# Seven block products in place of eight for the last half of a shared expert, with weight sums on GpSimd

## Chip, cores and metric

The kernel runs on one core of one Trainium2 chip. The metric is the device time of one execution in microseconds; lower is better. All values are fp32; products run as fp32r with each operand split into a high and a low part.

## What is computed

An attention-like recurrence with layer norm, then a mixture of experts with a shared expert, then a layer norm again. The change lies in the shared expert's first matrix product, `x @ w_sh_gate_up`. There are 2048 tokens of 512 numbers and 8 experts, 2 of them for each token; the shared expert goes from 512 to 2 x 1024 (gate and up) and back to 512; `_silu_and_mul` is silu of the first half times the second.

```python
x = _layernorm(x + _L0_attn_ref(x, ...), axis=-1)
x = _layernorm(x + _L0_ffn_ref(x, ...), axis=-1)
...
gu = jnp.einsum('th,ehf->etf', x, w_gate_up)
act = _silu_and_mul(gu)
eo = jnp.einsum('eti,eih->eth', act, w_down)
routed = jnp.einsum('te,eth->th', combine, eo)
shared = _silu_and_mul(x @ w_sh_gate_up) @ w_sh_down
return (routed + shared).reshape(orig_shape)
```

## The kernel before

`stages()` writes out one plan, a list of steps; the five functions `sync`, `tensor`, `vector`, `scalar` and `gpsimd` each run through it and issue their own part of each step, so that every engine's queue has the plan's order. Semaphore waits by name (`on`) tie the engines together.

The tokens are 16 tiles of 128, in four groups q of 512. A unit w holds weights for 256 inner columns: gate columns and up columns of w_gate_up, 128 at a time (fc 0 and 1), and the matching rows of w_down. Units 0 to 3 are the shared expert for groups 0 and 1, then come 15 routed jobs (w = 4 to 18; eight of them full ones of 512 rows, seven strips that are run only if used), and units BASE to BASE+3 (w = 19 to 22) are the shared expert again, for groups 2 and 3.

A weight or activation x is split as high = fp32r(x) on ACT and low = x - high on DVE (gate weights, tokens, activations) or POOL (down weights); a product is three products, high*high, high*low, low*high (`TERMS`). For one unit and group, `gate` gives for each fc a gate half and an up half, each 4 contraction chunks x 3 terms = 12 products of 128x128 by 128x512 (L1181); `act` is silu on ACT (L1671), the multiply on DVE (L1454), the high part on ACT (L1673) and the low part on DVE (L1456). `down` is four tiles of 6 products (L1194), each added to the token tile in x1 by DVE (L1464). PSUM banks 0 to 3 take gate halves, 4 to 7 the down tiles.

The experts' results lie in DRAM (yd), stored by SP after a copy on ACT (L1724). For each token tile POOL fetches two rows per token by indirect DMA (`fetch`, L1828; two buffers, so fetch i+2 waits for join i), and DVE multiplies and adds them (`join`, two operations, L1512). `finish` takes the mean and variance (L1522, L1524 and three small POOL operations), `scale` applies them on ACT (L1729; the last tile on DVE, L1529), and SP stores the tile.

The end of the routed jobs: `rows_gate(14)` (w = 18, 48 products, L1268), in it the split of unit 19's gate weights (`split_gate`, L1652, L1444) after fc 0; one strip of `rows_down(13)`; twelve products of `gate(BASE, 2)`; `rows_down(14)` (24 products, L1305); then the eight unit and group pairs of `seq`, with joins and finishes from `jobs` between the gate's steps:

```python
    first = gate(BASE, 2)
    next(first)
    next(first)
    rows_down(JOBS - 1, iter(()))
...
            if step % 2 == 0:
                scale()
                if n in jobs:
                    (join if jobs[n][0] == "join" else finish)(jobs[n][1] + step // 2)
```

## Time and profile before

| | us |
|---|---|
| median of 3 runs (lowest, highest) | 688.53 (687.93, 689.41) |
| the profiled execution | 688.28 |
| its span, first to last instruction | 686.5 |

| engine | busy us | share | instructions |
|---|---|---|---|
| PE | 666.1 | 97% | 6828 |
| DVE | 425.4 | 62% | 745 |
| ACT | 294.3 | 43% | 510 |
| POOL | 294.3 | 43% | 308 |

PE is TensorE, DVE VectorE, ACT ScalarE, POOL GpSimd, SP the engine that issues most DMAs. A group of instructions is told by its source line, as L1194. A product's recorded duration (0.39 us for 512 columns) is longer than the distance between starts, since products overlap; what a product costs is read from the distance. The granted clock of TensorE is 1.00 where it runs at 2.4 GHz.

### The profile page before, as it was taken

To read this page: it belongs to the slowest core of one execution; us is meant where nothing else is said; L and a number is where in the kernel's file an instruction comes from. 1 tells how busy PE (TensorE), PEld (TensorE's weight loads), DVE (VectorE), ACT (ScalarE), POOL (GpSimd) and SP (SyncE) were. 2 spreads that over 40 slices of the span, in tenths; PEclk is the share of its full clock that TensorE was granted. 3 is DMA by queue.
4 is the path that set the end of the run, shared out by engine and by line. 5 is a ranking of instruction groups with operands and counts; after the bars stand their busy time and mean duration, and the time that the engine had idled before them with its cause. 6 is when DMAs were issued, how large, how long until landed. Compare 5 with 4: busy or idle time off the path is not lost.

```text
span 686.5 us, 16409 instructions
## 1 busy us (share of the span) xinstructions
PE 666.1 (97%) x6828; PEld 531.9 (77%) x6828; DVE 425.4 (62%) x745; ACT 294.3 (43%) x510; POOL 294.3 (43%) x308
## 2 busy tenths in 40 slices
PE   9999999999999999999999999999999999999994
PEld 7767777677777777787887888888887888888883
DVE  5875865876844464488946544554456267676655
ACT  5343444455454432531023656655667442142232
POOL 0747567667645431011015335533552244726232
PEclk9999999999999999999999999999999999999998
DMA  8213234232642441100064478676748765414222
GB/s 286 83 35 86 76 98 106 88 112 57 175 138 75 129 141 33 46 0 1 21 231 157 140 292 295 214 220 255 216 153 271 229 218 159 123 66 131 65 78 92
DMA packets 65998, 92.47 MB, mean 135 GB/s; under 512 B 16960, under 2 KB 32064, under 8 KB 65920
## 3 DMA queue, kind: packets, MB, share of 16 engines
q1 hardware_dynamic: 60240, 72.76, 32.2%
q0 software_dynamic: 5680, 18.62, 9.4%
q8 instruction: 56, 0.92, 0.6%
q14 instruction: 22, 0.18, 0.1%
HBM read 67.56 MB, written 23.79 MB: 133 GB/s over the span
## 4 chain that ended last, share of the span: by engine, by line
PE 67%; DVE 14%; POOL 8%; issue 6%; ACT 4%; DMA 1%; POOLq 0%; DVEq 0%; ACTq 0%
PE zbank L1181 8%; PE wbank L1181 7%; PE bank L1305 7%; PE bank L1194 7%; PE bank L1073 7%; PE zbank L1268 6%; PE wbank L1268 6%; PE bank L1128 4%; DVE x L1464 3%; PE zbank L1281 2%; PE bank L1181 2%; PE wbank L1107 2%; PE zbank L1091 2%; POOL za L1758 2%; DVE sg L1454 1%
## 5 line engine op out<-in xcount | busy, mean ns | idle before, releaser
L1790 POOL TENSOR_TENSOR xl<-RAW,xh 128x1024 fp32r<-128x1024 f32 x23 | 55.4, 2407 | 121.1 <-ACT xh L1657 120.9
L1673 ACT ACTIVATE ah<-sg 128x512 fp32r<-128x512 f32 x48 | 30.3, 632 | 157.4 <-DVE sg L1454 157.4
L1803 POOL DMA_INDIRECT xg<-x1d,idxu x39 | 42.1, 1079 | 71.2 <-DVE idxu L889 41.3
L1444 DVE TENSOR_TENSOR GL<-RAW,GH 128x1024 fp32r<-128x1024 f32 x42 | 50.3, 1223 | 11.2 <-ACT GH L1652 9.8
L1456 DVE TENSOR_TENSOR al<-sg,ah 128x512 fp32r<-128x512 f32 x48 | 34.2, 712 | 33.5 <-ACT ah L1673 33.5
L1194 PE MATMUL bank<-xh,ah 128*128 128x512 f32 x128 | 51.3, 401 | 2.3 <-DVE x L1464 1.9
L1828 POOL DMA_INDIRECT xg<-yd,SI x32 | 35.8, 1120 | 40.0 <-DVE x L1512 23.6
L1194 PE MATMUL bank<-xh,al 128*128 128x512 f32 x128 | 50.0, 390 | 0.0
L1194 PE MATMUL bank<-xl,ah 128*128 128x512 f32 x128 | 49.9, 390 | 0.0
L1073 PE MATMUL bank<-xh,GH 128*128 128x512 f32 x112 | 47.9, 427 | 0.8 <-DVE kS L1346 0.8
L1454 DVE TENSOR_TENSOR sg<-sg,zbank 128x512 f32<-128x512 f32 x22 | 15.1, 685 | 53.4 <-PE zbank L1268 36.4
L1652 ACT ACTIVATE GH<-RAW 128x1024 fp32r<-128x1024 f32 x44 | 45.2, 1056 | 0.0
L1464 DVE TENSOR_TENSOR x<-bank,x 128x512 f32<-128x512 f32 x64 | 40.9, 681 | 5.5 <-PE bank L1194 5.3
L1073 PE MATMUL bank<-xl,GH 128*128 128x512 f32 x112 | 44.1, 394 | 0.2
L1181 PE MATMUL zbank<-XH,GH 128*128 128x512 f32 x112 | 44.1, 394 | 0.2 <-DVE XL L1449 0.2
L1181 PE MATMUL wbank<-XH,GH 128*128 128x512 f32 x112 | 43.8, 391 | 0.0
L1073 PE MATMUL bank<-xh,GL 128*128 128x512 f32 x112 | 43.7, 390 | 0.0
L1181 PE MATMUL zbank<-XH,GL 128*128 128x512 f32 x112 | 43.6, 389 | 0.0
L1181 PE MATMUL wbank<-XH,GL 128*128 128x512 f32 x112 | 43.6, 389 | 0.0
L1181 PE MATMUL wbank<-XL,GH 128*128 128x512 f32 x112 | 43.6, 389 | 0.0
L1181 PE MATMUL zbank<-XL,GH 128*128 128x512 f32 x112 | 43.6, 389 | 0.0
L1512 DVE SCALAR_TENSOR_TENSOR x<-xg,WW,x 128x512 f32<-128x512 f32 x32 | 26.6, 841 | 14.3 <-DMA xg<-yd,SI 12.6
(301 smaller groups left out, 1753.6 us busy)
## 6 DMA issues: line engine op xcount, KB each, us to landing
RAW<-in_wgu SPq DMA_DIRECT2D x13, 1024.0 KB, 5.8
yd<-RAW SPq DMA_DIRECT2D x39, 256.0 KB, 5.2
RAW<-in_wsgu SPq DMA_DIRECT2D x14, 512.0 KB, 4.8
RAW<-in_wd SPq DMA_DIRECT2D x13, 512.0 KB, 5.8
xr<-in_xT SPq DMA_DIRECT2D x16, 256.0 KB, 4.7
x<-in_xtok SPq DMA_DIRECT2D x16, 256.0 KB, 4.2
x1d<-x SPq DMA_DIRECT2D x16, 256.0 KB, 2.5
RAW<-in_wsd SPq DMA_DIRECT2D x8, 512.0 KB, 4.5
```

The source lines that it names most:

```text
L1073: t = e.matmul(bank[b][:], (WL if wl else WH)[:, j, k, hg * 128:hg * 128 + 128], (xl if xlo else xh)[:, k, :], start=(k == 0 and not wl an ...
L1181: t = e.matmul(bank[b][:], (GL if wl else GH)[:, w % 2, k, c:c + 128], (XL if xlo else XH)[q % 2][:, k, :], start=(k == 0 and not wl and n ...
L1194: t = e.matmul(bank[b][:], (al if al_ else ah)[:, ap, k, j * 128:j * 128 + 128], (DL if wl else DH)[:, w % 2, k, :], start=(k == 0 and not ...
L1268: t = e.matmul(bank[b][:], (GL if wl else GH)[:, w % 2, k, c:c + 128], (rowl if xlo else rowh)[p][:, k, :], start=(k == 0 and not wl and n ...
L1305: t = e.matmul(bank[b][:], (al if al_ else ah)[:, p, k, h * 128:h * 128 + 128], (DL if wl else DH)[:, w % 2, k, :], start=(k == 0 and not ...
L1444: e.tensor_tensor(GL[:, w % 2, k:k + 2, :], gate_raw(w, k), GH[:, w % 2, k:k + 2, :].bitcast(F32), ALU.subtract).then_inc(*mark("low", "g" ...
L1456: e.tensor_tensor(al[:, ap, fc, :], sg[:, g, :], ah[:, ap, fc, :].bitcast(F32), ALU.subtract).then_inc(*mark("low", "a", w, q, fc))
L1464: e.tensor_tensor(x1[:, i, :], bank[b][:], x1[:, i, :], ALU.add).then_inc(*mark("acc", w, q, j))
L1652: e.activation(GH[:, w % 2, k:k + 2, :], gate_raw(w, k), ACT.Copy).then_inc(*mark("high", "g", w, k))
L1790: e.tensor_tensor(DL[:, w % 2, :, :], draw[:, raw_of(w), :, :], DH[:, w % 2, :, :].bitcast(F32), ALU.subtract).then_inc(*mark("low p", "d" ...
L1803: e.indirect_dma_start(place(s), None, x1d, bass.IndirectOffsetOnAxis(ap=idxu[:, LINES[s]:LINES[s] + 1], axis=0)).then_inc(*mark(f"dma xg{ ...
L1828: e.indirect_dma_start(xg[:, p, j, :], None, yd, bass.IndirectOffsetOnAxis(ap=SI[:, j, i:i + 1], axis=0)).then_inc(*mark(f"dma ya{p}", i, j))
```

## The change

Tokens of group 2 and 3, two halves of the contraction (chunks 0 and 1, 2 and 3), and gate and up columns form a 2 x 2 by 2 x 2 block product. It is computed by Strassen's scheme in Winograd's form, one block for each unit and fc (b = 0 to 7), with seven products of 2 chunks x 3 terms = 6 matmuls each (`SEVEN`: weight slot, token operand, bank, and whether it opens the bank) for what were eight.

- Token sums (T1 to T4, once): four differences and one sum of 1024 elements a partition on DVE (`pair sums`), high parts on ACT, low parts on DVE (`pair sums`, `pair splits`). Group 2's tokens are loaded again (`fetch pair`); group 3's are loaded one job earlier.
- Weight sums (four of 256 elements, for each block): on POOL (`mix sums`), high parts on ACT (`mix high`, `mix high sums`), low parts of plain weights on DVE and of sums on POOL (`mix low`). They take the place of `split_gate`.
- Result sums: the products accumulate in banks 0 to 3. Where a partial result is needed in two banks it is copied on ACT (`copy 1`, `copy 2`, `copy 5`), and DVE adds (`add 5`, `add 7`). `pair act` is `act` for both groups.
- `down` tiles go one by one between the products of a block (order 1, 5, 6, 2, 7, 3, 4; a tile after 5, 2, 3 and 4), a unit later; block 0 has the order 1, 2, 5, 6, 7, 3, 4 and lies among `rows_down(13)` and `rows_down(14)`, block 1 has no tiles among it. Joins and finishes are placed by `side`. Tiles 12 to 15 are finished before 8 to 11, and tile 11 is the last.
- Buffers are laid over others that are free by then; some activations of group 3 go to the y buffers (`y_done`).

```diff
+SEVEN = {1: (0, "B11", 0, True), 2: (1, "B21", 0, False), 3: (6, "B22", 1, False), 4: (2, "T4", 2, False),
+         5: (3, "T1", 3, True), 6: (4, "T2", 1, False), 7: (5, "T3", 2, False)}
...
                 if j + 1 < JOBS:
                     for _ in turn_rows(j + 1):
                         pass
-                split_gate(j + 5)
+                    split_gate(j + 5)
+                else:
+                    mix(0, gate_end[w - 1])
+                    do("pair sums")
+    mul_end, act_end = {}, {}
+    def mix(b, after):
+        do("mix sums", b, after)
+        do("mix high", b, after)
+        do("mix high sums", b)
+        do("mix low", b)
+    def block(b, order):
+        w, fc = BASE + b // 2, b % 2
+        for p in order:
+            do("mul", b, p, left[SEVEN[p][2]] if SEVEN[p][3] else None)
+            mul_end[b] = ("mul", b, p)
+            if p == 1:
+                do("copy 1", b, left[1])
+            elif p == 5:
+                do("copy 5", b)
+            elif p == 6:
+                do("copy 2", b, left[2])
+                do("add 5", b)
+            elif p == 2:
+                do("silu 2", b)
+                left[0] = ("silu", w, 2, fc)
+            elif p == 7:
+                do("add 7", b)
+            elif p == 3:
+                do("pair act", b, 3, ("down", w - 2, 3, 3) if b > 3 else None)
+                left[1], left[3] = ("silu", w, 3, fc), ("low", "a", w, 3, fc)
+            elif p == 4:
+                do("pair act", b, 2, ("down", w - 1, 2, 3) if b > 1 else None)
+                left[2] = ("low", "a", w, 2, fc)
+            yield p
+    def pair_down(u, q):
+        w = BASE + u
+        for j in range(4):
+            b, i = 4 + j, 4 * q + j
+            do("down", w, q, j, b, (2 if u % 2 else 1) if q == 3 else 0, left[b], acc.get(i))
+            acc[i] = left[b] = ("acc", w, q, j)
+            down_end[w] = ("down", w, q, j)
+            yield i
 
...
+        if j == JOBS - 3:
+            do("fetch pair")
         do("load down", j + 6)
         between = iter(())
         if ORDER[j] < FULL:
             rows_gate(j)
-            do("load gate", j + 7)
+            if j < JOBS - 1:
+                do("load gate", j + 7)
         else:
             between = rows_and_weights(j)
             next(between)
             strip_gate(j)
+            if j == JOBS - 2:
+                do("fetch tokens", 3, row_left[1], range(4))
             for _ in range(3):
                 next(between)
         if j == JOBS - 1:
-            do("fetch tokens", 3, row_left[1], range(4))
+            do("pair splits", gate_end[4 + j])
+            first = block(0, (1, 2, 5, 6, 7, 3, 4))
+            next(first)
         if j:
             rows_down(j - 1, between)
         if ORDER[j] >= FULL:
         split_down(j + 5)
 
 
-    first = gate(BASE, 2)
-    next(first)
-    next(first)
-    rows_down(JOBS - 1, iter(()))
-    seq = [(BASE + n, q) for n, q in ((0, 2), (0, 3), (1, 2), (1, 3), (2, 2), (3, 2), (2, 3), (3, 3))]
-    jobs = {1: ("join", 0), 2: ("join", 4), 3: ("finish", 0), 4: ("join", 8), 5: ("join", 12), 6: ("finish", 4), 7: ("finish", 8)}
...
+    def among():
+        yield
+        next(first)
+        yield
+        next(first)
+        yield
+    next(first)
+    rows_down(JOBS - 1, among())
+    mix(1, gate_end[4 + JOBS - 1])
+    split_down(BASE + 1)
+    do("load gate", BASE + 2)
+    do("load down", BASE + 2)
     do("fetch", 0)
     do("fetch", 1)
...
+    for _ in first:
+        pass
+    side = {1: (("join", 0), ("join", 1), ("join", 2)), 2: (("join", 3), ("join", 4), ("join", 5)),
+            3: (("join", 6), ("join", 7), ("finish", 0), ("finish", 1)), 4: (("join", 8), ("join", 9), ("finish", 2), ("finish", 3)),
+            5: (("join", 10), ("join", 11), ("join", 12)), 6: (("join", 13), ("join", 14), ("join", 15)),
+            7: (("finish", 4), ("finish", 5), ("finish", 6), ("finish", 7))}
+    for b in range(1, 8):
+        u = b // 2
+        downs = pair_down(u - 1, 2 + b % 2) if u else iter(())
+        jobs = iter(side[b])
+        for p in block(b, (1, 5, 6, 2, 7, 3, 4)):
+            if p == 1 and b < 7:
+                do("mix sums", b + 1, mul_end[b - 1])
+                do("mix high", b + 1, mul_end[b - 1])
+            if p == 1 and b in (4, 6):
+                split_down(BASE + u)
+            if p == 2 and b < 7:
+                do("mix high sums", b + 1)
+                do("mix low", b + 1)
+            if p in (1, 6, 2, 3):
                 scale()
...
+                kind, i = next(jobs, (None, 0))
+                if kind:
+                    (join if kind == "join" else finish)(i)
+            if p in (5, 2) or p in (3, 4) and b < 7:
+                next(downs, None)
+        if b == 2:
             do("load gate", BASE + 3)
             do("load down", BASE + 3)
...
+    scale()
+    for _ in downs:
+        pass
+    for i in pair_down(3, 3):
+        finish(i)
+        scale(keep=1)
+    for i in pair_down(3, 2):
         finish(i)
         scale(keep=1)
...
+                elif step == "mul":
+                    b, p, free = a
+                    s, name, to, opens = SEVEN[p]
+                    if free:
+                        e.wait_ge(*on(*free))
+                    if p in (1, 2):
+                        e.wait_ge(*on("low", "m", b, 0))
+                    elif p == 4:
+                        e.wait_ge(*on("low", "m", b, 2))
+                    else:
+                        e.wait_ge(*on("low p", "m", b))
+                    if b == 0:
+                        e.wait_ge(*(on("low", "f", 2, 3) if name in ("B11", "B21") else on("low", "pair", name)))
+                    if p == 6:
+                        e.wait_ge(*on("copied", b, 1))
+                    elif p == 2:
+                        e.wait_ge(*on("copied", b, 1))
+                    elif p == 7:
+                        e.wait_ge(*on("copied", b, 2))
+                    elif p == 3:
+                        e.wait_ge(*on("added", b, 5))
+                    elif p == 4:
+                        e.wait_ge(*on("added", b, 7))
+                    for k in range(2):
+                        for wl, xlo in TERMS:
+                            t = e.matmul(bank[to][:], mixed(GL if wl else GH, b, s)[:, k, :], tokens_of(name, xlo)[:, k, :],
+                                         start=(opens and k == 0 and not wl and not xlo), stop=True, skip_group_check=True)
+                    t.then_inc(*mark("mul", b, p))
...
+                elif step == "pair sums":
+                    q1, q2 = pairs_[:, 0, :, :], pairs_[:, 1, :, :]
+                    r1, r2, t2 = XL1_[:, 0:2, :], XL1_[:, 2:4, :], xg_[:, 1, :, :]
+                    e.wait_ge(*on("dma pair", 3))
+                    e.wait_ge(*on("dma xr1", 3, 3))
+                    e.tensor_tensor(q1, r1, q1, ALU.subtract).then_inc(*mark("pair sum", 1))
+                    e.tensor_tensor(q2, q2, r2, ALU.subtract).then_inc(*mark("pair sum", 0))
+                    e.wait_ge(*on("pair sum", 1))
+                    e.tensor_tensor(r1, r2, r1, ALU.subtract).then_inc(*mark("pair sum", 3))
+                    e.wait_ge(*on("turned", "r", len(LINES) - 1))
+                    e.tensor_tensor(t2, r2, q1, ALU.subtract).then_inc(*mark("pair sum", 2))
+                    e.wait_ge(*on("pair sum", 0))
+                    e.tensor_tensor(q2, q2, q1, ALU.add).then_inc(*mark("pair sum", 4))
+                    e.wait_ge(*on("high", "pair", "T3"))
+                    for name in ("B22", "T3"):
+                        e.tensor_tensor(tokens_of(name, True), r1 if name == "T3" else r2, tokens_of(name, False).bitcast(F32), ALU.subtract).then_inc(*mark("low", "pair", name))
+                elif step == "pair splits":
+                    for name, raw in (("T1", pairs_[:, 0, :, :]), ("T2", xg_[:, 1, :, :]), ("T4", pairs_[:, 1, :, :])):
+                        e.wait_ge(*on("high", "pair", name))
+                        e.tensor_tensor(tokens_of(name, True), raw, tokens_of(name, False).bitcast(F32), ALU.subtract).then_inc(*mark("low", "pair", name))
+                elif step == "add 5":
+                    b, = a
+                    e.wait_ge(*on("mul", b, 6))
+                    e.wait_ge(*on("copied", b, 2))
+                    e.tensor_tensor(bank[1][:], bank[1][:], turned[:], ALU.add).then_inc(*mark("added", b, 5))
+                elif step == "add 7":
+                    b, = a
+                    e.wait_ge(*on("mul", b, 7))
+                    e.wait_ge(*on("added", b, 5))
+                    e.tensor_tensor(bank[3][:], bank[2][:], turned[:], ALU.add).then_inc(*mark("added", b, 7))
...
+                elif step == "mix high":
+                    b, after = a
+                    e.wait_ge(*on(*gate_in(BASE + b // 2)))
+                    e.wait_ge(*on(*after))
+                    e.activation(mixed(GH, b, 0, 2), graw[:, raw_of(BASE + b // 2), :, 128 * (b % 2):128 * (b % 2) + 128], ACT.Copy).then_inc(*mark("high", "m", b, 0))
+                    e.activation(mixed(GH, b, 2), quarter(3, b), ACT.Copy).then_inc(*mark("high", "m", b, 2))
+                elif step == "mix high sums":
+                    b, = a
+                    e.wait_ge(*on("mixed", b, 4))
+                    e.activation(mixed(GH, b, 3, 4), mixed(GL_, b, 3, 4), ACT.Copy).then_inc(*mark("high", "m", b, 3))
+                elif step == "pair sums":
+                    e.wait_ge(*on("pair sum", 3))
+                    e.wait_ge(*on("gate", 4 + JOBS - 2, "r", 0, 1))
+                    for name in ("B22", "T3"):
+                        e.activation(tokens_of(name, False), XL1_[:, 0:2, :] if name == "T3" else XL1_[:, 2:4, :], ACT.Copy).then_inc(*mark("high", "pair", name))
+                elif step == "pair splits":
+                    gone, = a
+                    e.wait_ge(*on(*gone))
+                    e.wait_ge(*on("pair sum", 4))
+                    e.activation(tokens_of("T1", False), pairs_[:, 0, :, :], ACT.Copy).then_inc(*mark("high", "pair", "T1"))
+                    e.activation(tokens_of("T2", False), xg_[:, 1, :, :], ACT.Copy).then_inc(*mark("high", "pair", "T2"))
+                    e.wait_ge(*on("low", "pair", "T1"))
+                    e.activation(tokens_of("T4", False), pairs_[:, 1, :, :], ACT.Copy).then_inc(*mark("high", "pair", "T4"))
+                elif step == "copy 1":
+                    b, free = a
+                    e.wait_ge(*on("mul", b, 1))
+                    e.wait_ge(*on(*free))
+                    e.activation(bank[1][:], bank[0][:], ACT.Copy).then_inc(*mark("copied", b, 1))
+                elif step == "copy 5":
+                    b, = a
+                    e.wait_ge(*on("mul", b, 5))
+                    if b:
+                        e.wait_ge(*on("added", b - 1, 7))
+                    e.activation(turned[:], bank[3][:], ACT.Copy).then_inc(*mark("copied", b, 5))
...
+                elif step == "mix sums":
+                    b, after = a
+                    e.wait_ge(*on(*gate_in(BASE + b // 2)))
+                    e.wait_ge(*on(*after))
+                    s1, s2, s3, s4 = (mixed(GL_, b, 3 + n) for n in range(4))
+                    e.tensor_tensor(s1, quarter(2, b), quarter(3, b), ALU.add).then_inc(*mark("mixed", b, 1))
+                    e.tensor_tensor(s3, quarter(0, b), quarter(2, b), ALU.subtract).then_inc(*mark("mixed", b, 3))
+                    e.wait_ge(*on("mixed", b, 1))
+                    e.tensor_tensor(s2, s1, quarter(0, b), ALU.subtract).then_inc(*mark("mixed", b, 2))
+                    e.wait_ge(*on("mixed", b, 2))
+                    e.tensor_tensor(s4, quarter(1, b), s2, ALU.subtract).then_inc(*mark("mixed", b, 4))
+                elif step == "mix low":
+                    b, = a
+                    e.wait_ge(*on("high", "m", b, 3))
+                    e.tensor_tensor(mixed(GL, b, 3, 4), mixed(GL_, b, 3, 4), mixed(GH, b, 3, 4).bitcast(F32), ALU.subtract).then_inc(*mark("low p", "m", b))
```

## Rows read from the trace of the kernel before

**Rows 1.** Page, busy us (share of the span) and instructions of each engine.

```profile
PE 666.1 (97%) x6828; PEld 531.9 (77%) x6828; DVE 425.4 (62%) x745; ACT 294.3 (43%) x510; POOL 294.3 (43%) x308
```

**Rows 2.** Chain that ended last, in time: start us, us, what; around the hand-over.

```profile
535.11 5.45 PE wbank L1268 x24
540.70 2.81 PE zbank L1181 x12
543.51 5.44 PE bank L1305 x24
```

**Rows 3.** Timeline of DVE at the hand-over: start us, us, engine, line, operation, tiles.

```profile
535.22 0.69 DVE L1454 TENSOR_TENSOR sg<-sg,zbank 128x512 f32<-128x512 f32 x1 [4.46 <-PE zbank L1268]
536.60 0.69 DVE L1456 TENSOR_TENSOR al<-sg,ah 128x512 fp32r<-128x512 f32 x1 [0.70 <-ACT ah L1673]
...
540.66 0.69 DVE L1454 TENSOR_TENSOR sg<-sg,wbank 128x512 f32<-128x512 f32 x1 [0.75 <-PE wbank L1268]
```

**Rows 4.** Timeline of ACT at the hand-over.

```profile
536.48 1.99 ACT L1652 ACTIVATE GH<-RAW 128x1024 fp32r<-128x1024 f32 x2
...
551.18 0.60 ACT L1724 ACTIVATE RAW<-bank 128x512 f32<-128x512 f32 x1 [2.96 <-DMA yd<-RAW]
```

**Rows 5.** Groups by shape on DVE, 500 to 687 us: busy, mean ns, idle before.

```profile
L1444 DVE TENSOR_TENSOR GL<-RAW,GH 128x1024 fp32r<-128x1024 f32 x14 | 16.7, 1221 | 1.8 <-ACT GH L1652 1.6
...
L1504 DVE TENSOR_TENSOR al<-wbank,ah 128x256 fp32r<-128x256 f32 x2 | 0.9, 426 | 0.9 <-ACT ah L1718 0.9
```

**Rows 6.** Groups by shape on ACT, 500 to 687 us.

```profile
L1673 ACT ACTIVATE ah<-sg 128x512 fp32r<-128x512 f32 x21 | 13.3, 632 | 73.7 <-DVE sg L1454 73.7
...
L1724 ACT ACTIVATE RAW<-bank 128x512 f32<-128x512 f32 x15 | 9.2, 616 | 6.6 <-PE bank L1305 3.6 <-DMA yd<-RAW 3.0
```

**Rows 7.** Groups by shape on POOL, whole span.

```profile
L1790 POOL TENSOR_TENSOR xl<-RAW,xh 128x1024 fp32r<-128x1024 f32 x23 | 55.4, 2407 | 121.1 <-ACT xh L1657 120.9
...
L1752 POOL TENSOR_TENSOR xl<-xr,xh 128x512 fp32r<-128x512 f32 x2 | 2.5, 1276 | 1.2 <-ACT xh L1595 1.2
```

**Rows 8.** One line's instructions, L1512: duration ns min/median/max, first and last start.

```profile
L1512 DVE SCALAR_TENSOR_TENSOR x<-xg,WW,x x32: 743/752/2887, 561.8 to 641.0; 128x512 f32<-128x512 f32 x32
```

**Rows 9.** Timeline of POOL, 555 to 572 us.

```profile
555.92 1.13 POOL L1828 DMA_INDIRECT xg<-yd,SI  x1 [10.00 <-DMA yd<-RAW]
...
561.62 2.54 POOL L1790 TENSOR_TENSOR xl<-RAW,xh 128x1024 fp32r<-128x1024 f32 x1
565.85 1.23 POOL L1828 DMA_INDIRECT xg<-yd,SI  x1 [1.68 <-DVE x L1512]
567.38 0.94 POOL L1828 DMA_INDIRECT xg<-yd,SI  x1 [0.30 <-issue]
...
570.21 0.95 POOL L1828 DMA_INDIRECT xg<-yd,SI  x1 [0.30 <-issue]
```

**Rows 10.** Timeline of DVE, 561 to 573 us.

```profile
561.83 2.89 DVE L1512 SCALAR_TENSOR_TENSOR x<-xg,WW,x 128x512 f32<-128x512 f32 x1
...
571.08 1.61 DVE L1512 SCALAR_TENSOR_TENSOR x<-xg,WW,x 128x512 f32<-128x512 f32 x2 [2.00 <-DMA xg<-yd,SI]
```

**Rows 11.** Windows: stretch, us, busy (x) PE, PEld, DVE, ACT, POOL, clock, DMA, GB/s.

```profile
677.50:680.00 2.50, 0.00 (x0) 0.00 (x0) 1.82 (x5) 1.55 (x2) 1.66 (x6) 1.00 0.52 201
681.00:684.00 3.00, 0.00 (x0) 0.00 (x0) 0.00 (x0) 0.00 (x0) 0.00 (x0) 0.50 0.44 169
```

**Rows 12.** Timeline of PE at the kernel's start.

```profile
1.46 4.05 PE L1058 MATMUL bank<-colsum 128*128 128x128 f32 x20 [1.46 <-DVE colsum L1320]
...
5.96 0.49 PE L1073 MATMUL zbank<-xh,GL 128*128 128x512 f32 x1
6.29 0.40 PE L1073 MATMUL zbank<-xh,GH 128*128 128x512 f32 x1
```

**Rows 13.** Timeline of DVE at the end.

```profile
676.30 0.66 DVE L1464 TENSOR_TENSOR x<-bank,x 128x512 f32<-128x512 f32 x1
...
677.82 0.66 DVE L1464 TENSOR_TENSOR x<-bank,x 128x512 f32<-128x512 f32 x1
```

More of the change, by code:

```diff
@@ L540, in sb, with under @@
             return stack.enter_context(nc.sbuf_tensor(name, [128] + shape, dt))
+        def under(name, shape, dt=F32):
+            with ExitStack() as brief:
+                return sb(brief, name, shape, dt)
         pair = [ctx.enter_context(nc.psum_tensor(n, [128, 2, 512], F32)) for n in ("zbank", "wbank")]
@@ L1460, in vector @@
                     e.wait_ge(*on("down", w, q, j))
+                    if before and w > BASE:
+                        e.wait_ge(*on(*before))
                     if not before and j == 0:
```

128 lines of the change are left out of this document (91 added, 37 removed).

## The prediction

> **What bounds the kernel now.** I read the page's busy shares first, then the chain that ended last in order of time, then the timelines of DVE, ACT and POOL around the place where the experts end and the shared expert's last half begins, then the groups by shape for durations.
>
> TensorE is busy 97% of the span with 6828 products [rows 1]. In the last 137 us the chain runs almost wholly over PE: 24 products in 5.44 us, product after product [rows 2]. That is 0.2267 us each, so six products, one "block product" of the new scheme or one `down` tile, take 1.36 us; I call that T. The gates of the last expert (w = 18) end at 540.56, twelve gate products of unit BASE fill the time until the expert's `act` is ready, and `rows down` follows with no hole [rows 2]. DVE starts 0.11 us after the last product of a half [rows 2, 3]; an engine released by ACT or DVE starts within 0.05 us. So each product taken from PE is worth its 0.2267 us as long as no other engine's queue makes PE wait. The question is what the queues of ACT, DVE and POOL, which run strictly in the plan's order, do with the added work.
>
> **Part 1, the products.** Before, units BASE to BASE+3 take 48 gate products for each of two token groups: 8 x 48 = 384. After: 8 blocks x 7 x 6 = 336. `down` is the same (192), so 48 products go: 48 x 0.2267 = **-10.9 us**, all of it on PE's path. This is the whole gain.
>
> **Part 2, the hand-over from the last expert.** Inside `rows_gate(14)`, between `act` of fc 0 and `act` of fc 1, the split of BASE's gate weights is replaced by `mix(0)` and `pair sums`; then `pair splits` comes before `copy 1` of block 0. Product 2 of block 0 waits for `copy 1`. PE has only product 1 and one `rows down` strip before it. So PE waits for all that stands ahead of `copy 1` on ACT, and that waits for DVE in its turn. Step by step, each duration from its row:
> - DVE ends fc 0's `low` at 537.3 [rows 3]. ACT begins `mix high` at 536.5, where the weight split stood [rows 4]: 0.6, 0.4, and 1.05 for the sums (two of 1024 take 1.99 [rows 4]), to 538.4. DVE's own `mix low`: 0.7 and 0.4 [rows 3, 5], to 538.3.
> - DVE, `pair sums`: five subtractions or additions of 1024 elements, 1.22 each alone [rows 5], 1.14 when they overlap (my estimate from that row less the 0.09 by which DVE operations overlap): the third ends at 541.7, the fifth at 544.0. ACT copies B22 and T3 behind the third: to 543.7. DVE takes their low parts, 2.3: to 546.2.
> - Only now does DVE reach fc 1's multiply, which before it did at 540.7: 0.69 [rows 3], to 546.9. ACT's high part 0.63 [rows 6]: 547.5. `pair splits`: T1 high 1.05, 548.5; T1 low on DVE 1.23, 549.8; T4 high, which waits for it, 1.05, 550.8; `copy 1` 0.6 [rows 6], 551.4.
> - PE is through product 1 and the strip at about 542.1. It waits 9.3 us.
>
> In the same stretch POOL runs `mix low(0)`, a subtraction of 1024 elements, 2.4 us [rows 7], against DVE's `pair sums`. The trace has such a meeting: POOL's subtraction from 561.62 to 564.16, and a DVE operation with both inputs in SBUF that started at 561.83 and took 2.89 us where the median is 0.75; it ended 0.6 after POOL [rows 8 to 10]. So I add 2.4 us: **+11.7 us**, and PE goes on at R = 553.8. (Bounds 9.3 and 12.5, the latter if `mix sums(0)` too falls on DVE.) The Trainium skill, SBUF — State Buffer, section Who interferes with whom, states that a DVE instruction with two SBUF inputs contends with a GpSimd instruction that reads SBUF, the loser blocking wholly; by that rule, and the trace agrees (2.89 us against 0.75), moving the weight sums to GpSimd doesn't make them free for DVE. Without it this term would be 9.3.
>
> **Part 3, the first joins.** `side` puts join 0, 1, 2 into block 1, which has no `down` tiles: 7T = 9.5 us. On DVE, `add 5` of block 1 is queued behind join 0 and `add 7` behind join 2; product 3 waits for the first, product 4 for the second. Fetch 2 on POOL needs join 0, and POOL has `mix sums(2)` ahead of it. From R:
> - PE needs 7 products or tiles to end `rows down(14)`: R + 9.5. ACT's `mix high(1)`, after one of the y copies (0.6, [rows 6]), ends by R + 12.0; POOL `mix low(1)` 2.4 and `split down` 2.4: R + 16.8. The last y store lands sooner: before, its copy ran at 551.18 and the fetch began at 555.92 [rows 4, 9], here R + 14.4.
> - Four fetch issues take 5.3 us (565.85 to 571.16, [rows 9]), and a tile is usable 3.7 us after its second issue starts (567.38 to 571.08, [rows 9, 10]): join 0 can start at R + 21.7, POOL has issued fetch 1 at R + 22.1.
> - `mix sums(2)`: four operations of 256 elements. POOL takes 1.28 for 512 and 2.41 for 1024 [rows 7], hence about 0.71 for 256: 2.9 us; with join 0's two operations of 0.75 on the other side of the lock, R + 26.5. Fetch 2's second issue starts at R + 27.8, lands R + 31.4, join 2 to R + 33.0, `add 7` to R + 33.7.
> - Product 4 of block 1 is the 17th piece after R: 16T = 21.8. PE waits 33.7 - 21.8 = **+11.9 us**. Check on the trace: from the first fetch to join 2 my steps need 14.6 us, and before it was 555.92 to 571.08 = 15.2 [rows 9, 10], where other gate products covered it. Bounds: 9 (no lock, split and sums partly overlapped) and 14.
>
> **Part 4, the blocks with `down` tiles.** 11T = 15.0 us each. Most waits fit: a copy costs 0.11 + 0.6 + 0.05, under T, and DVE's `add` 0.11 + 0.69 + 0.05. What does not is again `add 7` behind the third join (blocks 2, 5, 6). From the block's start: `mix sums` and the join under the lock 4.5, second issue 1.3, landing 3.7, join 1.6, one `acc` 0.7, `add 7` 0.7 = 12.5 against 9T = 12.2 for product 4; in block 6 `split down` (2.4) stands ahead of the fetch as well. Block 2 starts with POOL in arrears. I take 1.5 + 0.3 + 2.7 = **+4.5 us** (0 to 9).
>
> **Part 5, TensorE's clock.** PE is done by 677.5; the granted clock is 1.00 until 680 and 0.50 (1.2 GHz) from 681 to 684 [rows 11]. Both long holes are longer than the time between. At the kernel's start PE is busy from 1.46, and the 512-column products of 5.96 and 6.29 still start 0.33 apart in place of 0.227 [rows 12]. Half speed over such a stretch costs at most 2.4 us. I take 2.0 for the first hole; the second return partly lies under block 2's join chain, 1.0: **+3.0 us** (0 to 4.8).
>
> **Part 6, the end.** Eight tiles are finished one by one in place of four. DVE needs 1.52 us a tile (676.30 to 677.82, [rows 13]), PE 1.36: 4 x 0.16 = **+0.6 us**. The last tile has the same steps behind it. SP's token fetch goes one job earlier, ahead of four y stores, by 1.9 us of issue; the next copies that need their slots are over 10 us later: nothing. The pair loads go when SP is idle between weight loads: nothing. The added sums need no PE.
>
> **Sum.** The profiled execution took 688.28 (span 686.5 and 1.8 around it), 0.25 under the median of 688.53, so I use 688.3: 688.3 - 10.9 + 11.7 + 11.9 + 4.5 + 3.0 + 0.6 = 709.1. I forecast **709.0 us**. All low bounds: 688.3 - 10.9 + 9.3 + 9 = 695.7; all high: 688.3 - 10.9 + 12.5 + 14 + 9 + 4.8 + 0.6 = 718.3.
>
> **The rivals.**
> - Only the hand-over stalls; joins and fetches keep ahead of PE, as they do now. For it: in the trace PE never waits for a join. Against: there the accumulations do not stand behind joins on DVE. Time: 688.3 - 10.9 + 11.7 + 2.0 + 0.6 = 691.7. Chance 0.08.
> - Faster. The mechanism: ACT and DVE do the token sums while PE is still in `rows_gate(14)`, so that `copy 1` follows product 1 at once and the join chain starts with the present lead. It decides at a total stall of 10.9 us: below that the change gains. The price left is about 3 us of short waits: 688.3 - 10.9 + 3 = 680.4. Against: those sums begin only after 538 and hold some 13 us of dependent work. Chance 0.07.
> - GpSimd as the bound. In a block with three joins POOL has 2.9 + 2.4 of arithmetic and 3 x 2.65 of fetches, 13.3 of 15.0 us, and DVE some 12 us; if their lock serializes most of it, each of three such blocks loses 4 us more: 721. Chance 0.05.
> - No lock between DVE and POOL: 709.1 - 2.4 - 1.5 - 1.0 = 704.2, inside my case (0.15 of its 0.80).
>
> **How the numbers follow.** The forecast case holds 0.80, from 695.7 to 718.3. The range reaches to the first rival, since the two large terms could each be one I mis-ordered: 691 to 719, leaving out the faster case and the GpSimd case, and the ends. A measurement of this kernel tells about 0.2% (1.4 us) from no change. Faster 0.07, same 0.02, slower 0.91.
>
> **What would show it.** After: 6780 products on PE. In the chain, a hole before block 0's product 2 of about 11 us that ends with ACT's `copy 1` (its releaser), DVE in `pair sums` until about 548, and fc 1's multiply some 8 us later than 540.7. A hole of about 12 us in block 1 before product 4, released by DVE's `add 7`, with join 2 just ahead of it and, before that, the fetch's landing. Granted clock 0.5 behind both. DVE operations with two SBUF inputs far over their medians where POOL computes. The prediction is wrong if PE goes on within 3 us of 542, or if joins stand idle-free ahead of the additions.

## The result, and the profile after the change

The kernel after takes **718.75 us** (median of 4 runs, 718.25 to 719.6) against 688.23 (687.93 to 689.41) before: a ratio of 1.044 [1.042, 1.046]. The change costs 30.5 us, where its 48 products fewer are worth 10.9. The forecast was 709.0, in a range from 691 to 719; the sign and the two main places were right. The size fell at the range's end, 0.4 us above the sum of all high bounds (718.3).

The page of after (engine, busy us, share, instructions; then the slices), against [rows 1]:

```profile
PE 663.9 (93%) x6780; PEld 528.3 (74%) x6780; DVE 453.7 (63%) x775; ACT 318.2 (44%) x551; POOL 336.5 (47%) x348
...
PE   9999999999999999999999999999993939997893
...
PEclk9999999999999999999999999999997888999997
```

PE has its 6780 products, and two slices at 3 tenths. The waits of PE (who waited for what: us in all, times, longest) hold them; before, no gate product of the last 140 us was on that list:

```profile
PE wbank L1333 <- DVE wbank L1645: 16.1, 4, 9.1
PE zbank L1333 <- ACT zbank L1896: 11.7, 2, 11.5
PE zbank L1333 <- DVE zbank L1640: 3.2, 1, 3.2
```

L1333 is the product, L1896 `copy 1`, L1640 `add 5`, L1645 `add 7`. The timeline of PE at the holes (start, us, line, what ended the idle time; a hole is counted from 0.2267 us after the start of the last product before it, so it is a little longer than its bracket, since a matmul's shown end reaches beyond that). The first hole is put at 11.4 us throughout, with its two 32-column matmuls counted as long as full ones, though they take some 0.15 together:

```profile
541.34 0.40 PE L1333 MATMUL zbank<-XH,GL 128*128 128x512 f32 x1
541.58 0.30 PE L1465 MATMUL bank<-ident 128*128 128x32 f32 x2
553.39 0.77 PE L1333 MATMUL zbank<-XH,GH 128*128 128x512 f32 x1 [11.51 <-ACT zbank L1896]
553.95 0.63 PE L1333 MATMUL zbank<-XL,GH 128*128 128x512 f32 x1
554.38 0.63 PE L1333 MATMUL zbank<-XH,GL 128*128 128x512 f32 x1
...
581.19 0.47 PE L1333 MATMUL zbank<-XH,GH 128*128 128x512 f32 x1 [3.19 <-DVE zbank L1640]
...
591.95 1.19 PE L1333 MATMUL wbank<-pairs,GH 128*128 128x512 f32 x2 [9.14 <-DVE wbank L1645]
...
657.91 0.59 PE L1333 MATMUL wbank<-pairs,GH 128*128 128x512 f32 x1 [4.61 <-DVE wbank L1645]
...
676.90 0.47 PE L1333 MATMUL wbank<-pairs,GH 128*128 128x512 f32 x1 [2.14 <-DVE wbank L1645]
```

**The hand-over** (first hole, 11.4 us). DVE there, in the order of the plan:

```profile
537.97 1.22 DVE L1621 TENSOR_TENSOR pairs_<-XL_,pairs_ 128x1024 f32<-128x1024 f32 x1
539.11 3.42 DVE L1622 TENSOR_TENSOR pairs_<-pairs_,XL_ 128x1024 f32<-128x1024 f32 x1
...
545.85 2.35 DVE L1631 TENSOR_TENSOR XL<-XL_,XH 128x1024 fp32r<-128x1024 f32 x2
548.12 0.68 DVE L1605 TENSOR_TENSOR sg<-sg,wbank 128x512 f32<-128x512 f32 x1
```

The pair sums run from 538 to 548.1, and only then comes fc 1's multiply, 7.5 us after its time in [rows 3]. The second sum took 3.42 us in place of 1.22: POOL's subtraction lay beside it, itself 3.19 in place of the 2.41 of [rows 7]. On ACT, behind fc 1's high part, T1's, T2's and T4's high parts follow, T4's after T1's low part, and `copy 1` starts at 552.66:

```profile
538.25 3.19 POOL L2067 TENSOR_TENSOR GL<-GL_,GH 128x1024 fp32r<-128x1024 f32 x1 [1.80 <-ACT GH L1878]
...
551.70 1.06 ACT L1891 ACTIVATE pairs<-pairs_ 128x1024 fp32r<-128x1024 f32 x1 [0.34 <-DVE RL L1635]
552.66 0.58 ACT L1896 ACTIVATE zbank<-zbank 128x512 f32<-128x512 f32 x1
```

**Block 1** (3.3 and 9.3 us). DVE goes join 0, `add 5`, join 1, then sits 3.85 us until fetch 2 has landed, joins, and adds:

```profile
578.12 2.31 DVE L1715 SCALAR_TENSOR_TENSOR x<-xg,WW,x 128x512 f32<-128x512 f32 x2 [4.39 <-DMA xg<-yd,SI]
580.36 0.69 DVE L1640 TENSOR_TENSOR zbank<-zbank,turned 128x512 f32<-128x512 f32 x1
...
587.62 3.58 DVE L1715 SCALAR_TENSOR_TENSOR x<-xg,WW,x 128x512 f32<-128x512 f32 x2 [3.85 <-DMA xg<-yd,SI]
591.11 0.69 DVE L1645 TENSOR_TENSOR wbank<-wbank,turned 128x512 f32<-128x512 f32 x1
```

POOL issued that fetch (second issue at 583.97) behind four weight sums, which took 4.3 us beside the joins; alone they were put at 2.9. Join 2 itself took 3.58 us in place of 1.60, with POOL's `mix low(2)` beside it from 587.43 to 589.78:

```profile
577.95 0.73 POOL L2058 TENSOR_TENSOR GL_<-RAW 128x256 f32<-128x256 f32 x1
...
581.09 1.20 POOL L2063 TENSOR_TENSOR GL_<-RAW,GL_ 128x256 f32<-128x256 f32 x1
...
583.97 0.95 POOL L2107 DMA_INDIRECT xg<-yd,SI  x1 [0.30 <-issue]
```

**Where the 30.3 us of span went** (716.8 less 686.5): hand-over 11.4; block 1 12.6; blocks 5 and 6 4.8 and 2.3; products slower than 0.2267 apart, and holes up to 0.5 us, 8.3 in all; the end 1.8 (from the last product to the last `scale` 5.28 us, 3.49 before); less 10.9. That adds to 30.3. The windows (stretch, us, busy and count of PE, PEld, DVE, ACT, POOL, granted clock, DMA share, GB/s) show the clock behind the holes, where before has 1.00 in both stretches:

```profile
553.40:562.00 8.60, 8.60 (x26) 6.87 (x27) 0.61 (x1) 3.28 (x6) 5.16 (x5) 0.67 0.18 68
592.00:600.00 8.00, 8.00 (x26) 6.41 (x27) 4.48 (x7) 3.18 (x6) 5.47 (x7) 0.71 0.25 68
```

### The profile page after: what moved, and what is told of

Same layout as the page of the kernel before. It is cut to its first block, busy times and chain, and to the rows that moved or that the text cites. A ratio compares the mean times of both kernels' runs of the same rounds, so it can differ in the third digit from the quotient of the medians.

```text
span 716.8 us, 16598 instructions
## 1 busy us (share of the span) xinstructions
PE 663.9 (93%) x6780; PEld 528.3 (74%) x6780; DVE 453.7 (63%) x775; ACT 318.2 (44%) x551; POOL 336.5 (47%) x348
## 4 chain that ended last, share of the span: by engine, by line
PE 64%; DVE 15%; POOL 8%; issue 7%; ACT 4%; DMA 1%; DVEq 0%; POOLq 0%; ACTq 0%
PE bank L1456 7%; PE bank L1345 7%; PE bank L1196 6%; PE zbank L1419 6%; PE wbank L1419 5%; PE zbank L1333 4%; PE bank L1251 4%; PE wbank L1333 4%; PE zbank L1304 3%; PE wbank L1304 3%; PE zbank L1432 2%; PE wbank L1230 2%; PE bank L1304 2%; PE zbank L1214 2%; POOL za L2020 1%
## 5 line engine op out<-in xcount | busy, mean ns | idle before, releaser
L1935 ACT ACTIVATE ah<-sg 128x512 fp32r<-128x512 f32 x32 | 20.2, 632 | 97.1 <-DVE sg L1605 97.1
L1595 DVE TENSOR_TENSOR GL<-RAW,GH 128x1024 fp32r<-128x1024 f32 x34 | 40.9, 1224 | 10.7 <-ACT GH L1855 9.3
L1345 PE MATMUL bank<-xh,ah 128*128 128x512 f32 x112 | 45.0, 402 | 2.0 <-DVE x L1667 1.8
L2107 POOL DMA_INDIRECT xg<-yd,SI x32 | 32.1, 1003 | 16.8 <-DVE x L1715 9.8
L1715 DVE SCALAR_TENSOR_TENSOR x<-xg,WW,x 128x512 f32<-128x512 f32 x32 | 31.7, 991 | 12.3 <-DMA xg<-yd,SI 10.6
L1607 DVE TENSOR_TENSOR al<-sg,ah 128x512 fp32r<-128x512 f32 x32 | 24.2, 756 | 22.3 <-ACT ah L1935 22.3
L1855 ACT ACTIVATE GH<-RAW 128x1024 fp32r<-128x1024 f32 x36 | 37.2, 1059 | 0.0
L1792 ACT ACTIVATE W<-wbank 128x512 f32<-128x512 f32 x31 | 18.5, 597 | 37.8 <-PE wbank L1230 37.8
L1538 DVE TENSOR_TENSOR r<-zbank,mask 128x256 f32<-128x256 f32 x31 | 13.0, 419 | 33.9 <-PE zbank L1214 33.6
L1333 PE MATMUL zbank<-XH,GH 128*128 128x512 f32 x48 | 19.9, 414 | 14.7 <-ACT zbank L1896 11.5
L2020 POOL TENSOR_TENSOR za<-r 128x512 f32<-128x512 f32 x16 | 24.4, 1523 | 18.3 <-ACT r L1785 16.5
L1230 PEld LDWEIGHTS wbank<-r,RAW 32*32 32x32 f32 x2048 | 22.3, 103 | 12.7 <-issue 11.3
```

What stands on the lines that cost most here:

```text
L1230: t = e.matmul(bank[2 + h][g:g + 32, pp * 64:pp * 64 + 64], KK[o:o + 32, par, 1, c:c + 32], r[o:o + 32, n // 2 % 2, n % 2, 256 * h + pp * ...
L1333: t = e.matmul(bank[to][:], mixed(GL if wl else GH, b, s)[:, k, :], tokens_of(name, xlo)[:, k, :], start=(opens and k == 0 and not wl and ...
L1345: t = e.matmul(bank[b][:], act_of(al if al_ else ah, ap, k)[:, j * 128:j * 128 + 128], (DL if wl else DH)[:, w % 2, k, :], start=(k == 0 a ...
L1595: e.tensor_tensor(GL[:, w % 2, k:k + 2, :], gate_raw(w, k), GH[:, w % 2, k:k + 2, :].bitcast(F32), ALU.subtract).then_inc(*mark("low", "g" ...
L1855: e.activation(GH[:, w % 2, k:k + 2, :], gate_raw(w, k), ACT.Copy).then_inc(*mark("high", "g", w, k))
```

## Experiments

Times are compared with the kernel before on the same chip (688.1 to 689.3), so 1 us between runs of different chips is not read.

**e1_fill**: what the clock costs. PE is kept busy with products into a bank that nobody reads.

```
+ for _ in range({(0, 2): 48, (1, 4): 38}.get((b, p), 0)):
+     e.matmul(bank[4][:], mixed(GH, b, 0)[:, 0, :], ..., start=True, stop=True)
  if free:
      e.wait_ge(*on(*free))
```

> The changed kernel, with 48 extra products on TensorE (into a bank that nobody reads) ahead of block 0's product 2 and 38 ahead of block 1's product 4, where PE stands idle for 11.4 and 9.3 us. Nothing else moves. Theory (the slow products behind the two holes, 0.43 us apart, are the lower granted clock): they start 0.227 apart again, 2.9 us are won behind the first hole and 2.3 behind the second: 713.5 us, granted clock 1.00 in both places. Rival (the slow products come from their operands or from the queues): the spacing stays at 0.43 and the time at 718.7.

Measured 715.51, ratio 1.038 [1.034, 1.042]. The product after the filled hole is at normal pace at once:

```profile
554.12 0.47 PE L1335 MATMUL zbank<-XH,GH 128*128 128x512 f32 x1 [0.55 <-ACT zbank L1898]
554.43 0.40 PE L1335 MATMUL zbank<-XL,GH 128*128 128x512 f32 x1
554.66 0.40 PE L1335 MATMUL zbank<-XH,GL 128*128 128x512 f32 x1
```

The same work between the first hole and the second takes 21.5 us in place of 24.2, and between block 1's long hole and block 5's 58.7 in place of 61.0: the clock took **2.7 and 2.3 us**. The unfilled holes keep their size (3.4, 4.8, 2.3). The profiled run as a whole is only 2.0 us shorter than after's. It reached the hand-over 0.7 later; the second filling outlasted `add 7` (done at 589.96, product 4 at 590.79) by 0.7; and behind block 6's hole of 2.3 us the products ran 0.43 apart from 674.5 to 677.5 (granted clock 0.66 from 675.6 to 679.0), which costs 1.4 us and is not there in after, behind the same hole. So a lower clock can follow short holes too, and filling two holes does not take its whole price away.

**e2_zero**: what POOL's subtraction does to DVE. The low part of the weight sums is set to zero, so it is left out of the output; POOL still writes it, but reads nothing.

```
- e.tensor_tensor(mixed(GL, b, 3, 4), mixed(GL_, b, 3, 4), mixed(GH, b, 3, 4).bitcast(F32), ALU.subtract)
+ e.memset(mixed(GL, b, 3, 4).bitcast(F32), 0.0)
```

> The changed kernel, with POOL's subtraction for the low part of the weight sums replaced by a fill with zeros of the same 1024 elements, which reads no SBUF (the low part of the weight sums is left out of the computation). Theory (POOL reading SBUF locks DVE operations with two SBUF inputs): the second operation of pair sums falls from 3.42 to 1.22 us, the first hole from 11.4 to about 9.2, the two long joins of 2.9 in blocks 1 and 5 to 0.75: about 712 us. Rival (POOL's low part costs DVE nothing, only the queue order counts): 3.42 stays or the time stays at 718. Rival (writing alone takes the port too): the same as now.

Measured 707.01, ratio 1.026 [1.020, 1.032]: 12 us less than after, five more than expected.

```profile
538.57 0.96 POOL L2067 MEMSET GL<- 128x1024 f32 x1 [1.75 <-ACT GH L1878]
...
539.45 1.22 DVE L1622 TENSOR_TENSOR pairs_<-pairs_,XL_ 128x1024 f32<-128x1024 f32 x1
```

The same DVE operation takes 1.22 us beside a POOL instruction that only writes. The hand-over's hole is 9.2 (9.3 was forecast without the lock), block 1's are 2.0 and 7.3, block 5's 0.8 in place of 4.8. So the lock's price is 2.2 us in the hand-over, as the prediction had it, but some 7 in the blocks, where it had 1.5 and 1.0 (the terms of its rival without a lock). The memset is shorter too (0.96 for 2.4 us of POOL), so the blocks' share is not all lock, and no run parts the two. The two runs lie 3.4 us apart (705.32 and 708.70). The Trainium skill, SBUF — State Buffer, section Who interferes with whom, has the conflict in the port pair that VectorE and GpSimd share; the runs agree, 1.22 beside a GpSimd operation that reads nothing and 3.42 beside one that reads two inputs.

**e3_joins**: joins moved. Block 1 has none ahead of its additions; in blocks 2 to 6 the one behind product 1 still stands ahead of `add 5` on DVE, which product 3 waits for, so the expectation's "none ... within the block" holds for `add 7` alone.

```
- side = {1: (("join", 0), ("join", 1), ("join", 2)), 2: ...
+ side = {1: {4: ("join", 0)}, 7: {...}}
+ for b in range(2, 7):
+     side[b] = {1: ("join", 3 * b - 5), 7: ("join", 3 * b - 4), 4: ("join", 3 * b - 3)}
```

> The changed kernel, only the joins placed otherwise: none before block 1's last product, then in each block one after product 1, one behind add 7, one behind the last act, so that none stands on DVE ahead of an addition that a product waits for within the block. Theory (the holes of blocks 1, 5 and 6, 19.7 us, and the clock they cost, 4.3, come from additions queued behind joins that wait for a fetch): about 695 us, the first hole unchanged at 11.4. Rival (the fetches themselves are the bound, 16 joins need their time wherever they stand): over 708 us, with holes in front of the last tiles.

Measured 711.46, ratio 1.032 [1.029, 1.035]. A miss by 16 us (695 expected); the time lies in the rival's range (over 708), though not with holes ahead of the last tiles alone. Block 1's two holes of 12.6 us went, for one of 2.8 at the head of block 2, but seven of 0.7 to 2.3 us stand in blocks 4 to 7, 9.4 in all, where after has 7.1 in two. One cause that the prediction had not named, here for the hole at the head of block 2: ACT's `mix high sums` waits for POOL's weight sums, which stand behind fetch issues, and token group 3's `silu` in `pair act` is queued behind it, with DVE's multiply behind that. (ACT waits there in six blocks, 19.5 us in all.) Timelines of POOL, ACT and DVE:

```profile
575.93 1.07 POOL L2107 DMA_INDIRECT xg<-yd,SI  x1 [0.30 <-issue]
577.02 0.75 POOL L2058 TENSOR_TENSOR GL_<-RAW 128x256 f32<-128x256 f32 x1
...
580.01 1.06 ACT L1878 ACTIVATE GH<-GL_ 128x1024 fp32r<-128x1024 f32 x1 [3.81 <-POOL GL_ L2063]
580.97 0.58 ACT L1921 ACTIVATE sg<-zbank 128x512 f32<-128x512 f32 x1
...
581.58 0.70 DVE L1651 TENSOR_TENSOR wbank<-sg,wbank 128x512 f32<-128x512 f32 x1 [3.92 <-ACT sg L1921]
```

**e4_hand**: the hand-over re-placed. The pair sums are cut into single steps (`s` a sum, `h` a high part, `l` a low part), placed behind `act` of fc 1 and between the `rows down` strips.

```
- mix(0, gate_end[w - 1]); do("pair sums")
+ mix(0, gate_end[w - 1])
...
+ pair("s1", "hT1", "s2")
  rows_down(JOBS - 1, among())    # among: hT2 lT1 lT2 s3 | hT3 s0 lT3 | s4 hB22 ...
```

> The changed kernel, only the hand-over placed otherwise: copy 1 directly behind block 0's product 1, the token sums and their splits cut into single steps and put behind the last expert's act, between its down tiles, and block 0's products 5 and 6 after the third of them; the down split of unit 19 after block 0. Theory (queue order makes the first hole of 11.4 us and costs 2.9 of clock): the hole falls under 2 us in sum, block 1's holes stay at 12 to 13: 704 us. Rival (DVE and ACT have too much work in the hand-over whatever the order): over 4 us of holes remain between 542 and 558: 709 or more.

Measured 714.37, ratio 1.037 [1.034, 1.040]: 10 us over the expectation. The hole of 11.4 became 6.5 in seven pieces, but block 1's grew to 5.5 and 8.3:

```profile
563.59 4.69 POOL L2065 TENSOR_TENSOR xl<-RAW,xh 128x1024 fp32r<-128x1024 f32 x2 [5.11 <-ACT xh L1876]
568.42 0.96 POOL L2120 DMA_INDIRECT xg<-yd,SI  x1
```

PE reaches block 1's first hole 7.0 us sooner than in after (570.7 against 577.6), but the first fetch, with two `down` splits ahead of it, only 4.8 (568.42 against 573.22), and PE leaves block 1's long hole 4.8 us sooner too (587.16 against 591.95). The rest of what the hand-over gives is waited for in block 1.

**e5_dve**: weight sums and low parts on DVE, so that POOL has only fetches and `down` splits. The plan's order is unchanged; the two branches move, word for word, from POOL's loop to DVE's.

```
- POOL: "mix sums" (4 x 256 elements), "mix low" (1024)
+ DVE:  "mix sums", and in "mix low" a third subtraction: tensor_tensor(mixed(GL, b, 3, 4), ...)
```

> The changed kernel, only that the weight sums (four operations of 256 elements a block) and the low parts of the sums (one of 1024) run on DVE in place of POOL; order of the plan unchanged. Theory (the first fetch and fetch 2 stand behind POOL's sums, and POOL's reads lock DVE's joins): fetch 0 starts about 2.4 us sooner, fetch 2 about 4.5 us sooner after join 0, block 1's holes fall from 12.7 to about 6, those of blocks 5 and 6 from 7.1 to about 2, the first hole stays at 11 to 12 (2.5 us more on DVE, 2.2 less of lock): about 705 us. Rival (GpSimd is a good place for the sums, DVE has no room for 2.6 us more in a block of 15): more holes in the blocks with joins, 718 or more.

Measured 716.04, ratio 1.040 [1.037, 1.043]: a miss against 705, and just under the rival's 718; its interval overlaps that of after. The hand-over's hole grew to 12.0, since DVE is what sets it; block 1's fell to 6.0, as expected, with one of 2.1 ahead of block 0's product 4; the later blocks have 8.9 us in holes of 0.5 to 3.1 where 2 were expected. So what the lock had cost seems to be taken back by the four sums of 0.42 and the subtraction of 1.22 us per block.

**e6_three**: the three together, with the pair steps begun inside `rows_gate(14)` but fc 1's multiply ahead of most, fetches 0 and 1 ahead of the `down` splits, and each `scale` behind a block's last `act`.

```
+ do("mix sums", 1, ...) ... do("mix low", 1)
+ do("fetch", 0)
+ do("fetch", 1)
  split_down(BASE)
  split_down(BASE + 1)
```

> All three causes taken away together: token sums cut into single steps and put where DVE and ACT are free, copy 1 directly behind product 1, fetches 0 and 1 ahead of the down splits; joins never ahead of an addition that a product of the same block waits for; weight sums and their low parts on DVE. The 48 products stay away. Theory (only queue order and the lock ate the gain): holes under 5 us in sum, the clock at 1.00 throughout, 688.5 - 10.9 + 4 + 1.8 at the end = about 683 us, faster than both kernels. Rival (DVE is the bound: some 14 us of its work in a block of 15, 1.52 us a tile at the end): 690 or more.

Measured 698.66, ratio 1.015 [1.013, 1.017]: 20 us better than after, 16 over the expectation, and in the rival's range (690 or more). No hole is over 2.4 us, but they sum to 16. The joins behind product 1 stand ahead of `add 5` here as in e3_joins. In blocks 4 and 6 a `down` split on POOL still meets a join (two operations, 1.60 us alone), with `add 5` of the block behind it (POOL and DVE in block 4):

```profile
612.24 2.42 POOL L2090 TENSOR_TENSOR xl<-RAW,xh 128x1024 fp32r<-128x1024 f32 x1
...
611.64 4.42 DVE L1756 SCALAR_TENSOR_TENSOR x<-xg,WW,x 128x512 f32<-128x512 f32 x2
```

**e7_nojoin**: after's schedule without the join chain. No fetches, and a join touches one column: the routed rows are left out of the output.

```
- do("fetch", 0); do("fetch", 1); ... do("fetch", i + 2)
- e.scalar_tensor_tensor(out=x1[:, i, :], in0=xg[:, i % 2, j, :], ...)
+ e.tensor_scalar(x1[:, i, 0:1], x1[:, i, 0:1], 1.0, None, ALU.mult)
```

> The changed kernel without the fetches and with each join cut to two operations on one column, so the routed experts' rows are never added (left out of the output). Theory: the holes of block 1 (13.3 us in all) and of blocks 2 to 6 (7.1) stand behind the chain of fetch, landing, join and addition, and the clock that follows them costs some 4.5 more; the hand-over hole of 11.4 us is no part of it. Then 718.7 - 13.3 - 7.1 - 4.5 = 694, with one long hole left near 542 and last product near 681. Rival: the blocks are held by the weight sums on GpSimd and the two copies and two additions of each block, joins or no joins; then over 705, and the holes of blocks 1, 5 and 6 stay with GpSimd's low parts as releaser.

Measured **691.82**, ratio 1.005 [1.003, 1.007]. This is the state of the prediction's first rival, "only the hand-over stalls" (691.7). One long wait is left:

```profile
PE zbank L1329 <- ACT zbank L1890: 11.7, 2, 11.5
...
PE wbank L1329 <- DVE wbank L1641: 0.3, 1, 0.3
```

So 26.9 of the 30.5 us hang on the joins and their fetches, and the weight sums and additions alone hold almost nothing up. But 2.6 of them are no stall: from the start of the last `scale` to the end of the span there are 3.5 us here, 6.1 in before and in after, because GpSimd's closing drain takes 3.9 us without these fetches and 6.5 with them. On equal terms the time is 694.4, so its match with 691.7 is luck. The run takes away DVE's joins, POOL's issues and the landings together, and doesn't say how much each of them costs.

**e8_three_nojoin**: the same cut in e6_three.

> The kernel with all three parts re-placed (698.7 us; 15.9 us of holes, 2.3 to 4.8 of slow clock) without fetches and with joins of one column, the routed rows left out of the output. Theory that VectorE's queue is what is left: joins are 16 x 1.6 us of it, so nearly all holes go and the time is 688.3 - 10.9 + 3 to 5 = 681 to 683. Rival: the hand-over, in which there is no join, holds most of the loss: 690 or more.

Measured 685.19, ratio 0.9955 [0.9935, 0.9974]. The expectation was 681 to 683; between the two theories, nearer to the first. The routed rows cost e6_three 13.5 us, 2.6 of them in the closing drain. It is 3.5 us faster than before, and without the drain's share 0.9: even with no join at all, 6.7 us of short holes between 541 and 572, further short waits and the longer end eat nearly all of the 10.9 us.

**e9_three_zero**: e6_three with the sums' low part a memset on DVE (left out of the output, as in e2_zero).

> The same kernel with joins, and the low parts of the weight sums set to zero by a memset on VectorE in place of a subtraction of 1024 elements (low parts of the sums left out of the output). If VectorE's time is the bound, eight times the difference of the two operations (some 0.7 us each, 5 us in all) comes off where it is on the path: 694 to 695. If the landing of the fetches is the bound, nothing: 698 to 699.

Measured 697.42, ratio 1.013 [1.010, 1.016]: 1.9 us under e6_three, each against before on its chip, and the two intervals overlap: inconclusive between the theories. The same holes of 2.3 and 2.2 us before `add 5` of blocks 4 and 6 stayed; the operation lies behind them.

**e10_downs**: e6_three with the last two `down` splits later, and their low parts on DVE.

```
- if p == 1 and b in (4, 6):
+ if p == 6 and b in (5, 7):
      split_down(BASE + u)
+ DVE, "split down", w > BASE + 1: tensor_tensor(DL[:, w % 2, :, :], draw[...], DH[...], ALU.subtract)
```

> The kernel with all three parts re-placed (698.7 us), with the last two units' down weights split later (blocks 5 and 7 in place of 4 and 6) and their low parts on VectorE. There each of GpSimd's two subtractions of 2.42 us stretched two join operations from 1.60 to 4.42 and 4.35 us, and behind them PE waited 2.34 and 2.18 us for the next addition. Theory that the shared port is what stands on the path: 2 x 2.8 us come off VectorE's queue there, two operations of 1.2 come back where it is later and partly free: 694 to 695, and the holes near 615 and 651 are under 0.5 us. Rival, the fetches' landing (3.7 us behind each second issue) sets the joins and so the additions: the same holes stay, released by the same addition behind a join that waits for the DMA: 698 to 699.

Measured **694.01**, ratio 1.008 [1.007, 1.010], as expected. The join beside no POOL arithmetic, and the whole line (min/median/max ns):

```profile
611.62 1.59 DVE L1761 SCALAR_TENSOR_TENSOR x<-xg,WW,x 128x512 f32<-128x512 f32 x2
```

```profile
L1761 DVE SCALAR_TENSOR_TENSOR x<-xg,WW,x x32: 739/748/754, 575.8 to 658.5; 128x512 f32<-128x512 f32 x32
```

In after the longest of these was 2916 ns, in before 2887 [rows 8]. DVE is never idle ahead of a join here, so the fetches' landing is not what is left there. Of the 12.3 us in holes over 0.5 us, 6.7 lie between 541 and 572, as in e8_three_nojoin. For the rest DVE's time is the likely cause. The same 75 us of before and then of e10_downs, where they reach from within block 3 to block 7 (DVE is the third busy column):

```profile
593.00:668.00 75.00, 75.00 (x332) 62.12 (x331) 50.39 (x84) 22.08 (x33) 32.43 (x50) 1.00 0.28 90
```

```profile
593.00:668.00 75.00, 70.15 (x301) 55.69 (x300) 66.66 (x114) 30.65 (x50) 30.62 (x43) 1.00 0.33 99
```

DVE is busy 67% of the stretch before and 89% here, in an order that PE waits for: 2.8 us for `add 7` in four blocks, 1.2 for low parts, 0.9 for a copy. No version that computes everything beats the kernel before. One was not tried: the scheme in the later units alone, with eight products in unit BASE, which would give the pair sums time at a saving of 8.2 us at most (six blocks of 1.36).

## Why the prediction was right, and where its sizes were off

The mechanism was right: 48 products fewer, and waits at the hand-over and behind the first joins that cost more than twice their worth. That 718.75 lies inside a range that ends at 719 is luck: it is above the sum of all high bounds, since the clock and the end came out over theirs.

- **Products, -10.9**: right: 6780 on PE, and PE is out of work by 541.7 (542.1 forecast).
- **Hand-over, +11.7**: 11.4, with PE resuming at 553.39 (553.8 forecast), released by `copy 1`, behind T4's high part. The lock's 2.4 us of it measured 2.2 (e2_zero). The alternative without it, 9.3, measured 9.2. PE starts 0.15 us after the end of `copy 1` (553.24) and of `add 7` (591.80), where the prediction put 0.05.
- **First joins, +11.9**: 12.6 for the two holes and 0.7 in small ones. The chain was as written: fetch landing, join 2, `add 7`. Join 0 could start at R + 21.7; it did at R + 24.7, as POOL reached the first fetch at 573.2, R + 19.8 (R + 16.8 forecast). The step put ACT's `mix high(1)` behind one y copy and ended it by R + 12.0; it ended at 568.3, R + 14.9, behind a y copy at 565.9. This lateness is the clock's: PE needed 12.5 us for `rows down(14)` and block 0's products in place of 9.5. The term hides it, since PE's own next product was late by the same 2.7 us. Join 2 then took 3.58 us in place of 1.6, a stretch by `mix low(2)` that is not in the sum; in e2_zero it took 1.61. The prediction also gave one hole where there were two, as `add 5` waits for join 0 by the same chain.
- **Blocks with `down` tiles, +4.5**: 7.1. Block 2 had no such hole (1.5 forecast), block 5 4.8 (0.3), block 6 2.3 (2.7). The step that failed is the lock on the join: it was priced on the sums ahead of the join, while POOL's `mix low` fell on the join itself in block 5 (two operations 3.77 us in place of 1.60), with `add 7` behind it. The stretch itself is 2.2 of the 4.8; e2_zero, where POOL's operation is also shorter, takes 4.0 away.
- **Clock, +3.0**: the mis-sized term. e1_fill gives 2.7 and 2.3 for the two long holes; the third, of 4.8 us, brought 0.57 in the window behind it and about 1.6 us. Forecast were 2.0 and 1.0: the bound of 2.4, taken from the kernel's start, was a little short, the second return did not lie under a join chain but was paid in full, and a third was not in the sum. In all 6.6 us, above the high bound of 4.8.
- **End, +0.6**: 1.8. DVE's pitch of 1.53 us per tile was as forecast (1.52), but the sum took four tiles' difference only; by eight tiles of 0.16 it is 1.3.
- **The rivals.** "Only the hand-over stalls" is the state that is left as soon as the joins go (e7_nojoin): the forecast rightly gave the joins more weight than the trace of before, in which PE never waits for one. "GpSimd as the bound", 721, lies about 2 us from the measured time, yet its loss of 4 us in each of three blocks came in block 5 alone (4.8). e5_dve empties POOL of the weight sums and gains 2.7 us, but it loads DVE in their place, so it is no clean test. "No lock" falls with e2_zero. "Faster" decides at a stall of 10.9 us in all; with every part re-placed the stalls are 16 to 21 us (e6_three, e10_downs), so none of the orders tried reaches it.

The experiments' own expectations failed in one way: e3_joins, e4_hand, e5_dve and e6_three each took a wait's length off the time. The queues of ACT, DVE and POOL are one chain through block 1 and on, and a part repaired alone is waited for again at the next place. e7_nojoin and e10_downs, which took work off the busiest queue's path, came out within 2.2 us (0.4 without the drain) and 1 us.

## What to carry to other kernels

Products saved on TensorE are paid for by the engines that prepare their operands: before such a trade, count what VectorE gets in added work per block; here it went from 67% to 89% of the time in its best version, and the saving was lost in waits. Look at what is queued ahead of each operation that releases TensorE (a join, a copy, a fetch issue), since that, far more than the operation's own length, made the long holes here. The repair of one wait is worth its length only if the next place on the same queues has slack, so measure with the next suspect taken out, and check what else goes with it: here 2.6 us of a closing drain.

## What the runs showed of the hardware

- A DVE operation with both inputs in SBUF is stretched by about POOL's remaining time, also when DVE's queue is without a gap: 1.22 to 3.42 us at the hand-over, 0.42 to 2.60 and 2.47 beside two POOL subtractions of 5.10 in e10_downs. POOL is stretched too, 2.41 to 3.19, and its sums of 256 elements 0.73 to 1.25.
- Beside a POOL memset DVE ran at its own pace (1.22).
- After a hole of 11.4 us products start 0.43 us apart for 5.7 us, at a granted clock of 0.67 over the window; with PE kept busy through the hole, 0.23 apart from the second one on. In e1_fill products also ran 0.43 apart behind holes of 3.4 and 2.3 us; in after they did not, behind holes of the same length.
- GpSimd's closing drain takes 6.5 us in before and after, and 3.9 in the two runs without the joins' fetches.
